# Layer 3's preparation as three f16 products, and layer 2's self loop added to the adjacency by GpSimd

## The reference, cut to what matters

```python
h = relu(layernorm(x)); x = x + L2(h)
h = relu(layernorm(x)); x = x + L3(h)

def L2(X):                                # the self loop is added once more
    adj_hat = adj + eye
    d = 1 / sqrt(sum(adj_hat, axis=1))
    return relu((adj_hat * d[:, None] * d[None, :]) @ (X @ W) + b)

def L3(x):                                # hyperbolic maps around two products
    h = h_add(exp_map(log_map(x) @ embed), embed_bias)
    neigh = exp_map(adj @ log_map(h))
    out = exp_map(log_map(concat(x, neigh)) @ layer)
    return h_add(out, layer_bias)
```

## Time and profile before

| what | before |
|---|---|
| median of 3 runs (lowest to highest) | 900.39 us (900.21 to 901.58) |
| the profiled execution: its own time, its span | 900.15 us, 898.4 us |
| PE busy, share of the span | 844.8 us, 94% |
| DVE busy | 644.3 us, 72% |
| ACT busy | 473.4 us, 53% |
| POOL busy | 290.0 us, 32% |
| mean granted TensorE clock | 0.989 of full speed |

### The profile page before, as it was taken

The page is one execution under the profiler, slowest core; times in us unless marked ns, Lnnn a source line. Parts: engine busy times, 40 slices in busy tenths (PEclk is TensorE's granted clock), DMA queues, the critical chain, the costliest instruction groups (busy, mean ns, idle before and its releaser), DMA issues.

```text
span 898.4 us, 18058 instructions
## 1 busy us (share of the span) xinstructions
PE 844.8 (94%) x6368; PEld 505.3 (56%) x6368; DVE 644.3 (72%) x1784; ACT 473.4 (53%) x987; POOL 290.0 (32%) x381
## 2 busy tenths in 40 slices
PE   0699999999999999999999999999999999999992
PEld 0366777777777777654444445554555555555441
DVE  6989999999999999962545434433147666637876
ACT  5878888887888887741111101101055665434543
POOL 6844444444554465531212100000022131213221
PEclk9899999999999999999999999999999999999997
DMA  8999999999999996000011100000000000000000
GB/s 264 225 220 265 240 267 234 291 227 246 266 268 258 238 255 119 2 1 7 18 24 23 24 1 1 1 1 1 0 1 1 1 1 1 1 1 24 24 24 24
DMA packets 104783, 91.87 MB, mean 102 GB/s; under 512 B 83072, under 2 KB 88320, under 8 KB 104704
## 3 DMA queue, kind: packets, MB, share of 16 engines
q1 hardware_dynamic: 101056, 90.20, 42.9%
q10 hardware_dynamic: 3648, 0.61, 0.4%
HBM read 69.81 MB, written 2.10 MB: 80 GB/s over the span
## 4 chain that ended last, share of the span: by engine, by line
PE 70%; DVE 16%; issue 6%; ACT 3%; DVEq 2%; POOL 2%; DMA 1%; ACTq 0%; SPq 0%; POOLq 0%
PE ps_acc L1374 28%; PE ps_acc L1293 16%; PE ps_s L1276 10%; PE ps_t L1374 6%; PE ps_t L1276 5%; DVE e_parts L806 3%; DVE ps_s L799 2%; POOL att_sb L398 1%; ACT e_parts L615 1%; DVE adj_t L738 1%; PE ps_s L1404 1%; PE ps_s L1436 1%; DMA x<-in_x 1%; DVE adj_t L755 1%; ACT ez L584 1%
## 5 line engine op out<-in xcount | busy, mean ns | idle before, releaser
L347 POOL CAST e_parts<-ez 128x512 f16<-128x512 f32 x256 | 158.8, 648 | 177.0 <-ACT ez L496 115.7
L1293 PEld LDWEIGHTS ps_acc<-h_a,e_parts 128*128 128x128 f16 x3072 | 185.9, 97 | 34.0 <-DVE e_parts L806 4.0
L1293 PE MATMUL ps_acc<-h_a,e_parts 128*128 128x129 f16 x3072 | 197.4, 219 | 2.3 <-DVE e_parts L806 2.1
L1374 PE MATMUL ps_acc<-adj_t,stage 128*128 128x512 fp8e4 x896 | 198.6, 379 | 0.0
L806 DVE TENSOR_TENSOR e_parts<-ez,e_parts 128x512 f16<-128x512 f32 x256 | 179.4, 740 | 1.0 <-POOL e_parts L347 1.0
L1374 PE MATMUL ps_acc<-adj_t,h_a 128*128 128x512 fp8e4 x768 | 169.0, 379 | 0.0
L584 ACT ACTIVATE ez<-x,small 128x128 f32 (+1 forms) x96 | 39.5, 482 | 202.8 <-DVE small L985 202.8
L1374 PEld LDWEIGHTS ps_acc<-adj_t,stage 128*128 128x128 f16 x896 | 87.1, 98 | 99.1
L1276 PE MATMUL ps_s<-u_t 128*128 128x512 f16 x534 | 132.9, 386 | 8.9 <-ACT ez L496 7.2
L471 ACT ACTIVATE bytes<-stage 128x1024 uint8<-128x1024 f32 x128 | 133.8, 1045 | 0.9 <-DVE x L767 0.6
L496 ACT ACTIVATE ez<-ps_s,scal 128x1024 f32<-128x1024 f32 x89 | 107.2, 1204 | 44.8 <-DVE ps_s L799 43.6
(11 more groups left out here) (161 smaller groups left out, 795.7 us busy)
## 6 DMA issues: line engine op xcount, KB each, us to landing
stage<-in_adj SPq DMA_DIRECT2D x128, 512.0 KB, 5.0
x<-in_x SPq DMA_DIRECT2D x4, 512.0 KB, 8.2
adj_t<-bytes SPq DMA_TRANSPOSE x128, 5.3
out<-x SPq DMA_DIRECT2D x8, 256.0 KB, 2.2
u_t<-e_parts SPq DMA_TRANSPOSE x16, 2.4
kernel_sb<-in_L_gnn_kernel ACTq DMA_DIRECT2D x1, 64.0 KB, 7.0
w_sb<-in_L_gnn_W ACTq DMA_DIRECT2D x1, 64.0 KB, 8.2
embed_top<-in_L_gnn_embed ACTq DMA_DIRECT2D x1, 64.0 KB, 8.3
```

The source lines that it names most:

```text
L347: g.tensor_copy(e_parts[:, HI, at, :], ez[:, at, :]).then_inc(ehi_done, 1)
L1293: last = t.matmul(att_acc[:, b, 0:D + 1], e_parts[:, re, g_s % RING, P * b:P * (b + 1)], h_a[:, s, rh, 0:D + 1], start=(s == 0 and n == 0 ...
L1374: last = t.matmul(acc, h[:, k, r, :], adj_f8[:, k // 2, CW * c:CW * (c + 1), k % 2], start=(k == 0 and r == LO), stop=(k == NB - 1 and r = ...
```

## The change

`turn_h` transposes the two halves apart, as f16, into one bank of PSUM (8 transposes; before, 8 products that summed the halves). `ht_evac` copies 1024 columns of f16 without a scale, where it copied 512 columns of f32. `prepare` makes three f16 products for each block (HI by HI, HI by LO, LO by HI) with a split copy of the two matrices, `embed16`, where it made one f32 product. `embed16` is made by two DVE instructions before layer 0's steps, and lives in unused columns of `att_sb`. The scale moves into `prep_evac`. The eight products with the identity are gone; GpSimd adds twice the identity to the four diagonal blocks of a chunk in layer 1 (`self_loops`, after that chunk's `rstd`), and subtracts it in layer 2 between the two kinds of roots of a pair. PE waits for these at the quarter q == c. The loops around the roots are written out.

```diff
-        ht_sb = bytes8[:, 1, :].bitcast(F32)
+        ht = bytes8[:, 1, :].bitcast(F16).rearrange("p (b r i) -> p b r i", b=BC, r=2)
...
-            with pool.Fori(0, NCH) as m:
+            def self_loops(m, op, done):
+
+                for b in range(BC):
+                    k = BC * m + b
+                    own = adj_f8[:, k // 2, P * k:P * (k + 1), k % 2]
+                    last = g.tensor_tensor(own, own, ident16x2[:, :], op, saturate=False)
+                last.then_inc(done, 1)
+
+            for m in range(NCH):
                 rstd(NCH + m)
+                pool.wait_ge(agg_done, NCH + m + 1)
+                self_loops(m, ALU.add, loop_in)
...
                 for par in (0, 1):
                     root_v(2 * i + par, par)
                 for par in (0, 1):
+                    pool.wait_ge(agg_done, 2 * NCH + 2 * i + par + 1)
+                    self_loops(2 * i + par, ALU.subtract, loop_out)
+                for par in (0, 1):
                     root(of_chunk(h2_sq, par), of_chunk(n_h2, par), h2_sq_in, n_h2_ok,
                          2 * i + par + 1)
...
-            with pool.Fori(0, NCH // 2 - 1) as i:
+            for i in range(NCH // 2 - 1):
...
-                a.activation(ht_sb, ps_t[:, 0, :], ACT.Copy, scale=1.0 / H_SCALE
-                             ).then_inc(ht_out, 1)
+                a.activation(ht.rearrange("p b r i -> p (b r i)"), ps_t[:, 0, :].bitcast(F16),
+                             ACT.Copy).then_inc(ht_out, 1)
...
+            v.tensor_scalar(embed16[:, HI, :, :], embed_top[:, :, :], W_SCALE, None, ALU.mult)
...
+            v.scalar_tensor_tensor(embed16[:, LO, :, :], embed_top[:, :, :], W_SCALE,
+                                   embed16[:, HI, :, :], ALU.mult, ALU.subtract
+                                   ).then_inc(embed_ok, 1)
...
-                if L == 2 and q == NB // BC - 1:
-
-                    for b in range(BC):
-                        for r in (LO, HI):
-                            t.matmul(acc[:, P * b:P * (b + 1)], h[:, BC * c + b, r, :],
-                                     ident16x2[:, :], start=False, stop=False,
-                                     skip_group_check=True)
+                if L >= 2 and q == c:
+
+                    pe.wait_ge((loop_in, loop_out)[L - 2], c + 1)
...
-                        last = t.matmul(ps_t[:, 0, P * b:P * (b + 1)], hs[:, b, r, :], ident16[:, :],
-                                        start=(r == LO), stop=(r == HI))
+                        last = t.transpose(turned[:, b, r, :], hs[:, b, r, :], ident16[:, :])
...
-                    last = t.matmul(prep_out2[:, b, :, :], ht_sb[:, P * b:P * (b + 1)],
-                                    embed_top[:, :, :], start=True, stop=True)
+                    for n, (rh, rw) in enumerate(((HI, HI), (HI, LO), (LO, HI))):
+                        last = t.matmul(prep_out2[:, b, :, :], ht[:, b, rh, :],
+                                        embed16[:, rw, :, :], start=(n == 0), stop=(n == 2))
```

More of the change, by code:

```diff
@@ L60 @@
 U_SCALE = 16384.0
+W_SCALE = 64.0
 B_SCALE = 16.0
@@ L165, in program @@
             hyp[:, n, :] for n in range(26))
+        embed16 = att_sb[:, :, :].rearrange("p b f -> p (b f)")[:, 26 * PB:26 * PB + 2 * D].bitcast(
+            F16).rearrange("p (r a f) -> p r a f", r=2, a=2)
         ps_s = ctx.enter_context(nc.psum_tensor("ps_s", [P, 4, CW], F32))
@@ L207, in program @@
                  "pow_in pow_ok hd_sum hd_hi hd_ok agg_done agg_out agg_turned w_done l_stats "
-                 "l_rstd l_scale l_relu l_split ht_ps ht_out prep_done bias_in hw_out x_done "
+                 "l_rstd l_scale l_relu l_split ht_ps ht_out embed_ok prep_done bias_in hw_out x_done "
                  "h_sq_in n_h_ok v_sq_in n_v_ok h2_sq_in n_h2_ok a_sq_in n_a_ok cat_sq_in "
-                 "n_cat_ok tanh_in tanh_out ln_in ln_out h2_ok v_ok v_out split_g beta_split beta_in "
+                 "n_cat_ok tanh_in tanh_out ln_in ln_out h2_ok v_ok v_out split_g loop_in loop_out beta_split beta_in "
                  "x_less x_att").split()
@@ L218, in program @@
          pow_in, pow_ok, hd_sum, hd_hi, hd_ok, agg_done, agg_out, agg_turned, w_done, l_stats,
-         l_rstd, l_scale, l_relu, l_split, ht_ps, ht_out, prep_done, bias_in, hw_out, x_done,
+         l_rstd, l_scale, l_relu, l_split, ht_ps, ht_out, embed_ok, prep_done, bias_in, hw_out, x_done,
          h_sq_in, n_h_ok, v_sq_in, n_v_ok, h2_sq_in, n_h2_ok, a_sq_in, n_a_ok, cat_sq_in,
-         n_cat_ok, tanh_in, tanh_out, ln_in, ln_out, h2_ok, v_ok, v_out, split_g, beta_split,
+         n_cat_ok, tanh_in, tanh_out, ln_in, ln_out, h2_ok, v_ok, v_out, split_g, loop_in, loop_out,
+         beta_split,
          beta_in, x_less, x_att) = (
@@ L625, in prep_evac @@
                 act.wait_ge(prep_done, m + 1)
-                a.activation(v0[:, BC * par:BC * (par + 1), :], prep_out2[:, :, 0, :], ACT.Copy
-                             ).then_inc(v_out, 1)
+                back = 1.0 / (H_SCALE * W_SCALE)
+                a.activation(v0[:, BC * par:BC * (par + 1), :], prep_out2[:, :, 0, :], ACT.Copy,
+                             scale=back).then_inc(v_out, 1)
                 squares(lambda b: prep_out2[:, b, 0, :],
-                        lambda b: v_sq[:, BC * par + b:BC * par + b + 1]).then_inc(v_sq_in, 1)
-                a.activation(hw[:, ds(BC * m, BC), :], prep_out2[:, :, 1, :], ACT.Copy
-                             ).then_inc(hw_out, 1)
+                        lambda b: v_sq[:, BC * par + b:BC * par + b + 1],
+                        scale=back).then_inc(v_sq_in, 1)
+                a.activation(hw[:, ds(BC * m, BC), :], prep_out2[:, :, 1, :], ACT.Copy,
+                             scale=back).then_inc(hw_out, 1)
             def ln_step(k, cut=PAIR):
@@ L1425, in turn_h @@
                 pe.wait_ge(l_split, NCH * L + m + 2)
+                turned = ps_t[:, 0, :].bitcast(F16).rearrange("p (b r i) -> p b r i", b=BC, r=2)
                 for b in range(BC):
                     for r in (LO, HI):
-                        last = t.matmul(ps_t[:, 0, P * b:P * (b + 1)], hs[:, b, r, :], ident16[:, :],
-                                        start=(r == LO), stop=(r == HI))
+                        last = t.transpose(turned[:, b, r, :], hs[:, b, r, :], ident16[:, :])
                 last.then_inc(ht_ps, 1)
@@ L1434, in prepare @@
                 pe.wait_ge(ht_out, m + 1)
+                if m == 0:
+                    pe.wait_ge(embed_ok, 1)
                 for b in range(BC):
-                    last = t.matmul(prep_out2[:, b, :, :], ht_sb[:, P * b:P * (b + 1)],
-                                    embed_top[:, :, :], start=True, stop=True)
+                    for n, (rh, rw) in enumerate(((HI, HI), (HI, LO), (LO, HI))):
+                        last = t.matmul(prep_out2[:, b, :, :], ht[:, b, rh, :],
+                                        embed16[:, rw, :, :], start=(n == 0), stop=(n == 2))
                 last.then_inc(prep_done, 1)
```

## The result

The changed kernel takes 902.08 us, the median of 20 runs (901.36 to 904.06), against 900.41 us for the kernel before (20 runs, 900.15 to 901.58, on the same chip). The ratio is 1.0019, 95% interval 1.0013 to 1.0025: slower by 1.67 us. The interval lies above 1, and the difference is just under the 1.8 us (0.2%) that the prediction takes for the least that can be told from no change.

What follows compares the result with a forecast made beforehand. It took PE (94% busy) and, in layer 2, a loop over ACT, GpSimd and DVE as near-equal bounds. -2.16 + 3 x 1.4 + 0.4 = +2.4 us gave 902.8 us in terms of the median, range 898.0 to 906.4.

Steps and rivals of the forecast that it cites:

- the loop: Layer 2's chain from prepare through ACT, GpSimd and DVE back to prepare: 35.16 us a pair of chunks.
- d: What GpSimd's subtractions cost the loop in one pair by holding DVE in `embed_begin`: 1.4 us taken, 0 to 3.5 possible.
- Two limits close together: Layer 2: PE's own 34.9 us a pair against the loop's 35.16, so PE's saved work turns into waiting at odd prepares.
- the rival in which PE's 7.0 us reach the end: The loop is no limit and PE's whole saving counts: 893.4 us, chance 0.05.
- About 2 us plus d: PE's expected wait for ACT's copy at each of prepare(3) and prepare(5).
- PE's terms: PE saves 8 x 0.45 us of identity groups and 8 x 0.43 us of shorter prepares, 7.0 us in all.
- The sum without d: What reaches the end from the shorter PE work and longer copy, without the subtractions' price: -2.16 us.
- the term of the shorter `prepare`: Layer 2's four odd prepares, three f16 products replacing one f32: 0.32 or 0.43 us less on the loop each time.
- The fourth pair's d: Between prepare(7) and `log_end`, where 1.0 us is to spare: only the excess over 1.0 counts, +0.4 us.
- The rule of the Trainium skill: DVE and GpSimd share SBUF ports under an exclusive lock; to the letter, d 1.0 or more, sum +0.8 us or more.
- The rival that GpSimd's instructions slip through: Short subtractions slip between DVE's steps in `embed_begin`, d under 0.2: 898.2 to 898.8 us, chance 0.20.

Runs made afterwards that it cites:

- e11_before_act_loop_out: The kernel before with ACT's loop over the pairs of layer 2 written out and nothing else: 899.70 us, ratio 0.9988.
- e1_no_loops: The changed kernel without GpSimd's additions and subtractions and PE's waits for them (layer 2's second self loop left out): 897.85 us, ratio 0.9969.
- e7_roots_there: The changed kernel without GpSimd's additions and subtractions, with three roots on four unused columns where a pair's eight subtractions stood: 897.51 us, ratio 0.9963.
- e4_moved: The changed kernel with a pair's eight subtractions issued between its two first roots, before `embed_begin`, and not after them: 897.53 us, ratio 0.9969.

## Why the prediction was right

The forecast was 902.8 us by the loop with d = 1.4, and 902.08 was measured. The mechanism came out as forecast, and two of its terms were mis-sized, both towards too long a time. The outcome lies near a line that the prediction drew: it gave 0.47 to a loss of more than 1.8 us and 0.33 to no change that can be told, and the loss is 1.67 us.

- *Two limits close together.* Right: `e11_before_act_loop_out` shows PE's limit at 34.65 us a pair (34.9 forecast), and the rival in which PE's 7.0 us reach the end fell: `e1_no_loops` gives back 2.7 us of them. "About 2 us plus d" of waiting at prepare(3) and (5) is 1.85 there and 1.14 at `weights`: PE meets the loop at two places, and the second was not foreseen.
- *PE's terms.* A `prepare` takes 660.04 - 658.73 = 1.31 us (1.30 forecast), the copy 1.028 (1.03).
- *d.* 1.25 us measured against 1.4, by the mechanism that was read from the earlier trace rows: DVE gets about one step through for each subtraction. Of the 1.4, 1.0 was worked out and 0.4 was a guess for steps that are caught one by one, so it is partly luck that 1.4 came out so near. One subtraction takes 0.43 us, eight in a row 3.12, 0.39 each (0.38 estimated).
- *The sum without d* was under-sized: -2.2 us in the text, 897.85 - 900.52 = -2.7 in `e1_no_loops`. Most of it is the term of the shorter `prepare` (0.32 at prepare(1) and (7), 0.43 at (3) and (5)). From its start to ACT's copy of its result it was 2.03 us at prepare(3) in the kernel before (706.04 to 708.07) and is 1.52 in `e1_no_loops`, 0.51 less; at prepare(1) it was 1.93 and is 1.52. That is 0.09 more than booked, four times. The rest, about 0.15 us, was not traced. This and the smaller d (three times 0.15) would make the forecast 1.0 us too high; it was 0.7 too high. Of the difference, 0.1 us is that the period of a pair grows by 36.35 - 35.07 = 1.28 us and not by 1.25; the rest is small against the scatter of the runs.
- *Layer 3.* The fourth pair's d was to be covered up to 1.0 us, which leaves 0.25 us of 1.25. PE's weight load does wait for DVE's rows, and twice, 0.54 us at 797.64 and 0.46 us at 799.51; the second wait was not foreseen. From the quarter behind prepare(7) to layer 3's first small product (line 1435, before 1415) it takes 802.98 - 778.44 = 24.54 us, against 801.41 - 777.24 = 24.17 us in the kernel before: the fourth pair costs 0.37 us, close to the 0.4 of the sum.
- *The rule of the Trainium skill.* The Trainium skill's page "SBUF — State Buffer", section "SBUF: two separate sides", lets a DVE instruction that has two SBUF inputs or runs in a two-port mode and a GpSimd instruction exclude each other. The subtractions agree in the main; the roots in `e7_roots_there` have two inputs, and do not hold DVE at all (0.17 us). Line 1118, with one tensor input of 8 columns, is held too (0.32 us), as was line 729 in the earlier trace rows; whether these run in a two-port mode no run here shows.
- *The rival that GpSimd's instructions slip through* has the right time for `e4_moved` (898.2 forecast, 897.5 measured) but not its cause: there DVE is waiting for ACT during most of the subtractions. Where it is not, in the changed kernel, its steps are caught.

## What to carry to other kernels

When work leaves the busiest engine, ask what the next limit is before counting the gain: here a loop over three other engines was already 0.5 us longer than PE's own work for a pair, and took most of it. GpSimd's elementwise work on 128 columns was cheap here only where DVE had no chain of short dependent steps to do; look for a place where DVE waits for another engine, and issue it there. Of a loop that sets the period, read every row on its way, table loads too: here one loop of the program written out was worth more (3.8 us) than the change under study.

## What the runs showed of the hardware that was not expected

- DVE's 8-column steps grow from 0.17 to between 0.31 and 0.46 us where GpSimd's 128-column fp8 subtractions catch them. The reciprocals keep their 0.20, and a step can pass unstretched (line 1093 in `e4_moved`, 0.17). Under roots of 4 columns nothing grows.
- With subtractions of 64 columns the same DVE steps took 4.43 us in two pairs and 5.1 to 5.2 us in the two others of one execution.
- An fp8 subtraction of 64 columns takes 0.27 us in a row (4.26 us for sixteen) and one of 128 columns 0.39: half the columns, a third less time.
- Writing out a loop of ACT with three passes removed five table loads of 1.28 us: the one ahead of the copy in each pass, and the one behind it in all but the first.
